# Two token tiles as one supertile, with the first MLP layers as seven block products in place of eight

## Chip, cores and metric

The kernel runs on one NeuronCore of one Trainium2 chip. The metric is the device time of one execution in microseconds (us). The figure to compare is the median of several runs.

## What is computed

The input x has 64 sequences of 64 tokens, 512 wide: 4096 tokens. Two layers follow each other. Cut to what matters:

```python
# layer 0: attention inside a sequence, then two MLPs of hidden width 2048
q, k, v  = x @ Wq, x @ Wk, x @ Wv
attn     = softmax((q @ k.T) * 512 ** -0.5)
attn_out = (attn @ v) @ Wp + bp
cms_out  = gelu(attn_out @ cW1 + cb1) @ cW2 + cb2 + one_hot(target)
modifier = gelu(concat([attn_out, cms_out]) @ mW1 + mb1) @ mW2 + mb2
x        = clip(x + cms_out + modifier, 0, 1)
# layer 1: an adapter 512 -> 256 -> 512, its weights chosen by the role of the sequence
y   = x + gelu(x @ W_down[role] + b_down[role]) @ W_up[role] + b_up[role]
out = layernorm(y) * gamma[role] + beta[role]
```

`cW1` is 512 x 2048, `mW1` 1024 x 2048, `cW2` and `mW2` are 2048 x 512. All is float32.

## The kernel before

**Numbers.** Every float32 operand of a large product is split in two fp32r parts, hi (a rounding, made by ACT) and lo (what is left, made by DVE). One product of 128 x 128 weights with 512 columns is then three matmuls: hi x hi, hi x lo and lo x hi (`mm3`, lines 1132 to 1134). So everything that PE multiplies must first pass ACT and then DVE.

**Start.** Wq Wk^T and Wv Wp are multiplied once, into eight blocks of weights. A tile's queries are then x times the first product, and the attended rows (before attention is complete they are called y) times the second give attn_out.

**Tiles.** The tokens go in eight tiles of 512. A tile has a stage A (queries of the next tile or attended rows: `project`, 4 x 4 x 3 matmuls each), a stage C (the `c` MLP) and a stage M (the `m` MLP). In C and M a loop goes over the 16 blocks `j` of 128 hidden rows: `half_step` multiplies one block of the first layer into one of the two banks `hb`, ACT takes gelu out of it twice (lines 569, 570), DVE makes the low half (line 879), and one step later `second_layer` adds the block to the four banks `acc`. The first layer takes 16 x 4 x 3 = 192 matmuls in C, 384 in M; the second 192 in each.

**Attention.** A tile has four pieces of 128 tokens (two sequences each). The steps of one piece are `scores`, the sums and the maximum of a row (`row_max`, lines 815 to 820), exp on ACT (line 530), the inverse and `p_norm` (lines 824, 826), `turn_p` (a transpose, line 1232), the split of it (lines 540, 835) and of the piece's keys `xk` (lines 536, 830), `values` (lines 1246, 1247), the sum over hi and lo (`y_sb`, line 840) and the split of y (lines 545, 846). For the next tile these steps are spread over the 16 steps of stage M, one step of a piece after each block `j`, four blocks to a piece. Only for tile 0 do they stand together: there the matmuls of Wv Wp (`product2`, 12 per piece) lie between them.

**Order.** Each engine has its own queue, written out by hand; the queues meet at counting semaphores only. An engine that waits lets nothing pass it. SP issues the weight loads, one block of 256 KB at a time into rings of `w1_st` (4) and `w2_st` (2). POOL issues x, xk and the store of z (line 448, once a tile). The weights of layer 1 are loaded and split under the last stage M (lines 601, 922). The last stage takes 34 pairs of sequences with the same role; the last tile's sequences come late in that order (`LATE`), since their z is stored last.

## Time and profile before

| | us |
|---|---|
| three runs | 2171.19, 2176.46, 2174.29 (median 2174.29) |
| the profiled execution | 2170.89 |
| its span, first to last instruction | 2169.0 |
| PE busy, of 9948 matmuls | 2140.1 |
| PE weight loads | 1780.6 |
| DVE busy | 1066.2 |
| ACT busy | 1045.0 |
| mean granted clock of PE | 0.997 of full |

The profile shows one execution. Busy time of PE is counted from a matmul's start to its modelled end, and matmuls overlap, so the spacing of starts is the price of one, not its duration (0.39 us for 512 columns). DVE and ACT overlap their operations a little too: the spacing of two starts in a full queue is below the duration. "Idle before, <-" names what ended a wait.

### The profile page before, as it was taken

The page shows a single profiled execution, that of the slowest core. Times are in us where ns is not written, and L with a number is a line of the kernel's source. Part 1 is how long each engine was busy: PE and PEld are TensorE (multiplying, and loading weights), DVE is VectorE, ACT ScalarE, POOL GpSimd, SP SyncE. Part 2 cuts the span into 40 slices and gives each one's busy share as a digit, 9 for nine tenths or more (in the row PEclk, how much of TensorE's full clock was granted, in tenths as well). Part 3 has the DMA queues.
Part 4 walks back from the last instruction along what each step waited for, and adds up shares of the span by engine and source line. Part 5 has one row for each costly group of instructions (what it writes and reads, how often), then busy time and mean ns, then how long its engine had stood idle before and what let it go on. Part 6 is the DMA issues. An engine that isn't in the chain of part 4 may idle for free.

```text
span 2169.0 us, 30587 instructions
## 1 busy us (share of the span) xinstructions
PE 2140.1 (99%) x9948; PEld 1780.6 (82%) x9949; DVE 1066.2 (49%) x1919; ACT 1045.0 (48%) x1929; POOL 75.4 (3%) x141
## 2 busy tenths in 40 slices
PE   7999999999999999999999999999999999999997
PEld 6788888888888888888888888888888888888886
DVE  6545444454435445454445445454545444354687
ACT  5545444454444545454445444454444444444564
POOL 1000000000000000000000000000000000000132
PEclk9999999999999999999999999999999999999999
...
DMA packets 126935, 247.84 MB, mean 114 GB/s; under 512 B 16653, under 2 KB 25360, under 8 KB 124112
## 3 DMA queue, kind: packets, MB, share of 16 engines
...
q14 instruction: 48, 0.39, 0.1%
...
## 4 chain that ended last, share of the span: by engine, by line
PE 95%; SPq 2%; issue 1%; DVE 1%; ACT 1%; DMA 0%; POOL 0%; ACTq 0%; POOLq 0%; DVEq 0%
PE hb L1132 19%; PE hb L1134 19%; PE hb L1133 19%; PE acc L1132 11%; PE acc L1134 11%; PE acc L1133 11%; PE scores L1224 1%; PE yb L1246 1%; SPq L356 1%; SPq L357 1%; SPq L365 0%; SPq L362 0%; PE yb L1247 0%; PE scores L1223 0%; PE acc L1378 0%
## 5 line engine op out<-in xcount | busy, mean ns | idle before, releaser
L879 DVE TENSOR_TENSOR h_lo<-hf,h_hi 128x512 fp32r<-128x512 f32 x256 | 177.2, 692 | 527.6 <-ACT hf L570 527.6
L569 ACT ACTIVATE h_hi<-hb,bias_sb 128x512 fp32r<-128x512 f32 x256 | 176.4, 689 | 483.7 <-PE hb L1134 483.6
L1132 PE MATMUL hb<-a_hi,w_hi 128*128 128x512 f32 x1024 | 403.9, 394 | 0.0
L1132 PE MATMUL acc<-h_hi,w_hi 128*128 128x512 f32 x1024 | 401.0, 392 | 0.2 <-DVE h_lo L879 0.2
L1134 PE MATMUL hb<-a_hi,w_lo 128*128 128x512 f32 x1024 | 399.5, 390 | 0.0
L1134 PE MATMUL acc<-h_hi,w_lo 128*128 128x512 f32 x1024 | 399.2, 390 | 0.0
L1133 PE MATMUL hb<-a_lo,w_hi 128*128 128x512 f32 x1024 | 398.9, 390 | 0.0
L1133 PE MATMUL acc<-h_lo,w_hi 128*128 128x512 f32 x1024 | 398.6, 389 | 0.0
L802 DVE TENSOR_TENSOR w_lo<-w_st,w_hi 128x512 fp32r<-128x512 f32 x256 | 177.1, 692 | 322.5 <-ACT w_hi L516 322.5
L516 ACT CAST w_hi<-w_st 128x512 fp32r<-128x512 f32 x254 | 157.8, 621 | 358.5 <-PE acc L1134 358.5
L797 DVE TENSOR_TENSOR w_lo<-w_st,w_hi 128x512 fp32r<-128x512 f32 x448 | 296.3, 686 | 17.0 <-ACT w_hi L511 14.0
L511 ACT CAST w_hi<-w_st 128x512 fp32r<-128x512 f32 x448 | 262.8, 618 | 9.1 <-issue 8.4
L1134 PEld LDWEIGHTS hb<-a_hi,w_lo 128*128 128x128 f32 x1024 | 192.3, 188 | 41.1
L1134 PEld LDWEIGHTS acc<-h_hi,w_lo 128*128 128x128 f32 x1024 | 192.3, 188 | 40.5
L1132 PEld LDWEIGHTS hb<-a_hi,w_hi 128*128 128x128 f32 x1024 | 192.4, 188 | 39.9
L1132 PEld LDWEIGHTS acc<-h_hi,w_hi 128*128 128x128 f32 x1024 | 192.2, 188 | 39.7 <-DVE h_lo L879 1.0
L1133 PEld LDWEIGHTS acc<-h_lo,w_hi 128*128 128x128 f32 x1024 | 192.4, 188 | 39.1
L1133 PEld LDWEIGHTS hb<-a_lo,w_hi 128*128 128x128 f32 x1024 | 192.5, 188 | 37.6
L1132 PE MATMUL hb<-c_hi,w_hi 128*128 128x512 f32 x512 | 199.7, 390 | 0.2 <-DVE c_lo L955 0.2
L1133 PE MATMUL hb<-c_lo,w_hi 128*128 128x512 f32 x512 | 199.4, 389 | 0.0
L1134 PE MATMUL hb<-c_hi,w_lo 128*128 128x512 f32 x512 | 199.4, 389 | 0.0
L570 ACT ACTIVATE hf<-hb,bias_sb 128x512 f32<-128x512 f32 x256 | 174.4, 681 | 0.0
...
## 6 DMA issues: line engine op xcount, KB each, us to landing
w_st<-w1m SPq DMA_DIRECT2D x256, 256.0 KB, 2.8
w_st<-w1c SPq DMA_DIRECT2D x128, 256.0 KB, 2.8
w_st<-w2c SPq DMA_DIRECT2D x128, 256.0 KB, 2.7
w_st<-w2m SPq DMA_DIRECT2D x128, 256.0 KB, 2.6
...
xr<-xT POOLq DMA_DIRECT2D x8, 1024.0 KB, 5.6
```

What stands on the lines that cost most here:

```text
L356: b = sp.value_load(table[0:1, bass.ds(n, 1)], min_val=0, max_val=B - 1)
L357: sp.dma_start(zs[:, slot, k, :, :].rearrange("p c s -> p (c s)"), z_dram[bass.ds(b, 1)].rearrange("o p f -> (o p) f")).then_inc(zl[slot], 16)
L511: nc.scalar.copy(w1_hi[:, k % W1_RING, :], w1_st[:, k % W1_STAGE, :]).then_inc(w1_hi_s, 1)
L516: nc.scalar.copy(w2_hi[:, k % W2_RING, :], w2_st[:, k % W2_RING, :]).then_inc(w2_hi_s, 1)
L569: nc.scalar.activation(h_hi[:, j % 2, :], hb[j % 2][:], ACT.Gelu, bias=bcol(col + j))
L570: nc.scalar.activation(hf[:, j % 2, :], hb[j % 2][:], ACT.Gelu, bias=bcol(col + j)).then_inc(h_hi_s, 1)
L797: nc.vector.tensor_tensor(w1_lo[:, k % W1_RING, :], w1_st[:, k % W1_STAGE, :], f32(w1_hi[:, k % W1_RING, :]), ALU.subtract).then_inc(w1_lo ...
L802: nc.vector.tensor_tensor(w2_lo[:, k % W2_RING, :], w2_st[:, k % W2_RING, :], f32(w2_hi[:, k % W2_RING, :]), ALU.subtract).then_inc(w2_lo_ ...
L879: nc.vector.tensor_tensor(h_lo[:, j % 2, :], hf[:, j % 2, :], f32(h_hi[:, j % 2, :]), ALU.subtract).then_inc(h_lo_s, 1)
L1132: nc.tensor.matmul(ps, w[0], x[0], start=first, stop=False)
L1133: nc.tensor.matmul(ps, w[0], x[1], start=False, stop=False)
L1134: return nc.tensor.matmul(ps, w[1], x[0], start=False, stop=last)
```

## The change

Two tiles of 512 tokens (1 and 2 of the program's names) become a **supertile** of 1024; there are four. Weights of both MLPs are loaded, split and used once per supertile. The whole order is written out; before, seven of eight tiles were a loop.

**Seven products.** Take the first layer as a product of 2 x 2 blocks: the weights by hidden half and input half, the input by input half and tile. The four blocks of the result need eight block products, or seven by the scheme of Strassen and Winograd: each of the seven multiplies a *form* (a sum or difference) of weight blocks by a form of input blocks, and sums of the products give the four blocks. A **quad** `Q` is 2 hidden blocks x 2 tiles; there are 8 in a stage (`NQ`). Its seven products `P1` to `P7` have 2 x 3 matmuls each in stage C and 4 x 3 in M. P2 is added to P1's bank, P4 to P7's and P3 to P5's by PE itself; P4 and P3 wait until DVE has read those banks.

**New work.** Per quad DVE makes four sums of weight blocks (`weight_sums`), seven low halves of weights (`split_q`), five sums of products (`sum_p6`, `sum_p7`, `block22`, `block21`, `block12`), four low halves of gelu (`hidden_lo`), and four additions into `f2` (`part`). The `part`s are there because PSUM has eight banks: four hold the second layer of tile 1 (`TB`), four hold the products (`GB`), and the second layer of tile 2 uses the product banks at a quad's end and is added up in SBUF. Per stage, 14 forms of the input are built from eight blocks: eight differences (`difference`) and splits (`form`). In stage C they are `a_forms`, in stage M both `a_forms` and `c_forms`. cms_out goes out to DRAM and comes back (`cf_dram`, `z_cms`), for want of room.

**Attention** no longer lies under stage M. It stands alone at the head of each supertile: eight pieces in a row, with one `project` (12 matmuls) between two pieces, first the queries of tile 2, then the attended rows of tile 1. The attended rows of tile 2 (`attended2`) follow the last piece.

**Layer 1's weights**: `split_l1` waits for the last P3; the load of `wu` waits for the split of `wd`. `LATE` covers two tiles.

The core of the diff (DVE's `weight_sums` and `quad`, then PE's `attention` and quads):

```diff
+NQ = JH // 2
+OB = (0, 2, 1, 3)
+
+
+P1, P5, P7, P6, P2, P4, P3 = range(7)
+
+FORM = (0, 2, 4, 5, 1, 3, 6)
+
+BANK = (0, 3, 2, 1, 0, 2, 3)
+
+RHS = {P1: (0, 2), P2: (1, 3), P3: (4, 8), P5: (5, 9), P7: (6, 10), P6: (7, 11), P4: (12, 13)}
+NF = 14
...
+            def weight_sums(Q):
+
+                cols = width(Q // NQ)
+                a11, a12, a21, a22, s3, s2, s4 = [wr[:, k, cols] for k in range(7)]
+                dve.wait_ge(raw_in, raw_done(Q))
+                nc.vector.tensor_tensor(s3, a11, a21, ALU.subtract).then_inc(sums_s, 1)
+                nc.vector.tensor_tensor(a21, a21, a22, ALU.add).then_inc(sums_s, 1)
+                dve.wait_ge(sums_s, 4 * Q + 2)
+                nc.vector.tensor_tensor(s2, a21, a11, ALU.subtract).then_inc(sums_s, 1)
+                dve.wait_ge(sums_s, 4 * Q + 3)
+                nc.vector.tensor_tensor(s4, a12, s2, ALU.subtract).then_inc(sums_s, 1)
...
+            def quad(Q):
+
+                q = Q % NQ
+                if q >= 2:
+                    part(Q - 2, 3)
+                if q:
+                    for j in range(2):
+                        split_w2(Q - 1, j)
+                if q == 0:
+                    sum_p6(Q)
+                    sum_p7(Q)
+                    block22(Q)
+                split_q(Q, P3)
+                if (Q + 1) % NQ or Q // NQ % 2 == 0:
+                    weight_sums(Q + 1)
+                if q:
+                    hidden_lo(Q - 1, C22)
+                    hidden_lo(Q - 1, C12)
+                split_next(Q, 0)
+                if q:
+                    sum_p6(Q)
+                    sum_p7(Q)
+                    block22(Q)
+                split_next(Q, 1)
+                split_next(Q, 2)
+                block21(Q)
+                hidden_lo(Q, C11)
+                split_next(Q, 3)
+                block12(Q)
+                hidden_lo(Q, C21)
+                split_next(Q, 4)
+                split_next(Q, 5)
+                if q:
+                    for i in range(3):
+                        part(Q - 1, i)
...
+            def attention(s):
+                m0 = 2 * NP * s
+                for c in range(DC):
+                    query(s, c)
+                scores(m0)
+                between(s, 0)
+                for m in range(2 * NP):
+                    turn_p(m0 + m)
+                    if m + 1 < 2 * NP:
+                        scores(m0 + m + 1)
+                    if m == NP - 1:
+                        values(m0 + m)
+                    between(s, m + 1)
+                    if m != NP - 1:
+                        values(m0 + m)
+                    if s == 0 and m == 1:
+                        sort_counts()
+                    if s == 0 and m == 4:
+                        sort_gather()
+                for j in range(DC):
+                    attended2(s, j)
+
...
+            def product(Q, k, js):
+                g = Q // NQ
+                nk = 4 if g % 2 else 2
+                bank, w = GB[g % 2][BANK[k]], ring_q(Q, k)
+                first = k in (P1, P5, P7, P6)
+                for j in js:
+                    x = forms[j // 2]
+                    i = RHS[k][j % 2]
+                    ins = mm3(bank[:], ring(w, j), (x[:, i, 0, :], x[:, i, 1, :]), first and j == 0, j == nk - 1, not first)
+                if js[-1] == nk - 1:
+                    ins.then_inc(prod[k], 1)
+
+            def quad(Q):
+
+                g, q = divmod(Q, NQ)
+                js = range(4 if g % 2 else 2)
+                old = Q - 1
+                for k, seen in ((P1, (gelu_s, 4 * old + C11 + 1)), (P5, (sum_s, 5 * old + 5)),
+                                (P7, (sum_s, 5 * old + 4)), (P6, (sum_s, 5 * old + 1))):
+                    pe.wait_ge(w1_lo_s, ring_q(Q, k) + 1)
+                    if q == 1:
+                        pe.wait_ge(*seen)
+                    else:
+                        pe.wait_ge(part_s, 4 * (Q - 2) + BANK[k] + 1)
+                    product(Q, k, js)
+                second1(old)
+                add_products(Q, js)
+                second2(old, Q)
...
+            def add_products(Q, js):
+
+                for k, seen in ((P2, (p1_s, Q + 1)), (P4, (sum_s, 5 * Q + 2)), (P3, (sum_s, 5 * Q + 3))):
+                    pe.wait_ge(w1_lo_s, ring_q(Q, k) + 1)
+                    pe.wait_ge(*seen)
+                    product(Q, k, js)
...
+            def second2(Q, Q_now):
+
+                g = Q // NQ
+                pe.wait_ge(hlo_s, 4 * Q + 4)
+                seen = ((gelu_s, 4 * Q_now + C11 + 1), (sum_s, 5 * Q_now + 1), (sum_s, 5 * Q_now + 4), (sum_s, 5 * Q_now + 5))
+                for j in range(2):
+                    for i in range(4):
+                        if j == 0 and Q_now != Q:
+                            pe.wait_ge(*seen[i])
+                        elif j == 0:
+                            pe.wait_ge(part_s, 4 * (Q - 1) + i + 1)
+                        ins = second_layer(GB[g % 2][i], j, OB[i], (h2_hi[:, j, :], h2_lo[:, j, :]), j == 0, j == 1)
+                        if j:
+                            ins.then_inc(t2_mm, 1)
+                    if j == 0:
+                        ins.then_inc(t2_half, 1)
+
+            def first_quad_c(s):
+                Q, g = 2 * NQ * s, 2 * s
+                pe.wait_ge(w1_lo_s, ring_q(Q, P1) + 1)
+                form_ready(g, 2)
```

**Order of the instructions.** First PE, around the values of a piece. Before (in the loop, stage M; `hb` is the first layer's bank, `acc` the second layer's):

```order
L1132 MATMUL hb<-c_hi,w_hi 128x512
L1133 MATMUL hb<-c_lo,w_hi 128x512
L1134 MATMUL hb<-c_hi,w_lo 128x512
L1240 REGISTER_ALU [waits xk_lo_split,pt_lo_ready]
L1246 MATMUL yb<-pt_hi_lo,xk_hi 128x256 [waits y_lo_ready]
L1247 MATMUL yb<-pt_hi_lo,xk_lo 128x128
L1246 MATMUL yb<-pt_hi_lo,xk_hi 128x256
L1247 MATMUL yb<-pt_hi_lo,xk_lo 128x128
L1206 REGISTER_ALU
L1132 MATMUL acc<-h_hi,w_hi 128x512 [waits h_lo_ready]
```


After, piece 3 of the first supertile, from its transpose (`p_norm`) to the first attended row of tile 1 (x and y are the two sets of four banks):

```order
L1614 MATMUL x<-ident,p_norm 128x128 [waits p_normalised]
L1626 MATMUL x<-pt_hi_lo,xk_hi 128x256 [waits y_lo_ready,xk_lo_split,pt_lo_ready]
L1627 MATMUL x<-pt_hi_lo,xk_lo 128x128
L1626 MATMUL x<-pt_hi_lo,xk_hi 128x256
L1627 MATMUL x<-pt_hi_lo,xk_lo 128x128
L1626 MATMUL x<-pt_hi_lo,xk_hi 128x256 [waits y_lo_ready]
L1627 MATMUL x<-pt_hi_lo,xk_lo 128x128
L1626 MATMUL x<-pt_hi_lo,xk_hi 128x256
L1627 MATMUL x<-pt_hi_lo,xk_lo 128x128
L1508 MATMUL y<-x_hi_lo,w_hi 128x512 [waits w1_lo_split,y_lo_ready,a_t1_f32,form_lo]
```


The first-layer matmuls ahead of the values and the second layer behind them are gone; transpose, values and the next projection follow each other directly, each with a wait.

DVE in attention, before, one piece of tile 0 (L840 sums y, L835 and L830 split pt and xk, L815 to L820 row sums and maximum):

```order
L846 TENSOR_TENSOR y_lo<-y_sb,y_hi 128x2x128 [waits y_hi_ready] x2
L824 RECIPROCAL rinv<-rs 128x1 [waits exp_done]
L826 TENSOR_SCALAR p_norm<-p_exp,rinv 128x128 [waits row_inverse]
L840 TENSOR_REDUCE y_sb<-yb 128x256 [waits y_mm]
L840 TENSOR_REDUCE y_sb<-hb 128x256 [waits y_mm]
L835 TENSOR_TENSOR pt_hi_lo<-scores,pt_hi_lo 128x128 [waits pt_hi_ready]
L830 TENSOR_TENSOR xk_lo<-xk_st,xk_hi 128x512 [waits xk_hi_split]
L815 TENSOR_REDUCE s_sb<-hb 64x64 [waits scores_mm]
L815 TENSOR_REDUCE s_sb<-hb 64x64
L818 TENSOR_REDUCE mx<-s_sb 128x1 [waits scores_summed]
```


After, between pieces 4 and 5 of the first supertile (L1222 the low half of an attended row, L1202 sums y, L1009 to L1014 the weight sums, L1196 and L1191 pt and xk, L1176 row sums):

```order
L1187 TENSOR_SCALAR p_norm<-p_exp,rinv 128x128 [waits row_inverse]
L1222 SCALAR_TENSOR_TENSOR a_forms<-y,bias_sb,a_forms 128x512 [waits a_t1_f32,form_hi]
L1202 TENSOR_REDUCE y_sb<-x 128x256 [waits y_mm] x2
L1009 TENSOR_TENSOR w_blocks<-w_blocks 128x256 [waits blocks_loaded]
L1010 TENSOR_TENSOR w_blocks<-w_blocks 128x256
L1012 TENSOR_TENSOR w_blocks<-w_blocks 128x256 [waits weight_sums]
L1014 TENSOR_TENSOR w_blocks<-w_blocks 128x256 [waits weight_sums]
L1196 TENSOR_TENSOR pt_hi_lo<-x,pt_hi_lo 128x128 [waits pt_hi_ready]
L1191 TENSOR_TENSOR xk_lo<-xk_st,xk_hi 128x512 [waits xk_hi_split]
L1176 TENSOR_REDUCE s_sb<-x 64x64 [waits scores_mm]
L1176 TENSOR_REDUCE s_sb<-x 64x64
```


One low half and, in this piece, four weight sums now stand in the queue ahead of pt, xk and the row sums.

DVE in the MLP, before, two steps of stage C in the loop (L797 and L802 weights, L807 x, L879 the low half of gelu):

```order
L807 TENSOR_TENSOR x_hi_lo<-x_st,x_hi_lo 128x512 [waits x_hi_split]
L796 REGISTER_ALU
L797 TENSOR_TENSOR w_lo<-w_st,w_hi 128x512 [waits w1_hi_split]
L878 REGISTER_ALU
L879 TENSOR_TENSOR h_lo<-hf,h_hi 128x512 [waits h_hi_ready]
L801 REGISTER_ALU
L802 TENSOR_TENSOR w_lo<-w_st,w_hi 128x512 [waits w2_hi_split]
L806 REGISTER_ALU
```


After, the second half of a quad's queue in stage C and the start of the next (L982 a weight form, L1086 and L1090 `block21` and `block12`, L1061 the low half of gelu, L1035 `part`, L1018 w2):

```order
L1035 TENSOR_TENSOR f<-x,f 128x512 [waits t2_part_added,t2_part_mm] x4
L1018 TENSOR_TENSOR w_lo<-w_st,w_hi 128x512 [waits w2_hi_split] x2
L982 TENSOR_TENSOR w_lo<-w_blocks,w_hi 128x256 [waits w1_hi_split]
L1009 TENSOR_TENSOR w_blocks<-w_blocks 128x256 [waits blocks_loaded]
L1010 TENSOR_TENSOR w_blocks<-w_blocks 128x256
L1012 TENSOR_TENSOR w_blocks<-w_blocks 128x256 [waits weight_sums]
L1014 TENSOR_TENSOR w_blocks<-w_blocks 128x256 [waits weight_sums]
L1061 TENSOR_TENSOR h_lo<-f,h_hi 128x512 [waits gelu_ready] x2
L982 TENSOR_TENSOR w_lo<-w_blocks,w_hi 128x256 [waits w1_hi_split]
L1067 TENSOR_TENSOR p_copy<-p_copy,x 128x512 [waits product_mm_p6,p1_copied]
L1076 TENSOR_TENSOR f<-p_copy,x 128x512 [waits gelu_ready,product_mm_p7,block_sums]
L1081 TENSOR_TENSOR f<-f,x 128x512 [waits product_mm_p5,block_sums]
```


The fourth `part` of a quad is the first thing of a later quad's queue; it waits for the last matmul of the second layer.

## Rows read from the trace of the kernel before

**Rows 1.** The page: busy tenths of PE and its granted clock in 40 slices

```profile
PE   7999999999999999999999999999999999999997
...
PEclk9999999999999999999999999999999999999999
```

**Rows 2.** Timeline of PE, first projections (start us, us, engine, line, operation, idle before)

```profile
22.70 0.47 PE L1132 MATMUL hb<-x_hi_lo,w_hi 128*128 128x512 f32 x1 [2.14 <-DVE w_lo L797]
...
24.15 0.39 PE L1132 MATMUL hb<-x_hi_lo,w_hi 128*128 128x512 f32 x1
...
33.45 0.39 PE L1134 MATMUL hb<-x_hi_lo,w_lo 128*128 128x512 f32 x1
```

**Rows 3.** The store of z, one per tile: POOL line 448

```profile
L448 POOL DMA_DIRECT2D z_by_batch<-zb x7: 907/907/922, 327.5 to 1814.1; - x7
```

**Rows 4.** Timeline of PE, attention pieces of the first tile

```profile
43.60 0.29 PE L1232 MATMUL hb<-ident,p_norm 128*128 128x128 f32 x1
...
52.92 0.29 PE L1232 MATMUL hb<-ident,p_norm 128*128 128x128 f32 x1
55.70 0.55 PE L1246 MATMUL yb<-pt_hi_lo,xk_hi 128*128 128x256 f32 x1 [2.49 <-DVE y_lo L846]
...
58.90 0.77 PE L1132 MATMUL hb<-y_hi,w_hi 128*128 128x512 f32 x1 [1.26 <-DVE y_lo L846]
```

**Rows 5.** Timeline of DVE, the same stretch

```profile
43.34 0.69 DVE L840 TENSOR_REDUCE y_sb<-yb 128x256 f32<-128x512 f32 x1
...
44.87 0.69 DVE L830 TENSOR_TENSOR xk_lo<-xk_st,xk_hi 128x512 fp32r<-128x512 f32 x1
45.48 0.58 DVE L815 TENSOR_REDUCE s_sb<-scores 64x64 f32<-64x128 f32 x2
...
46.42 0.75 DVE L846 TENSOR_TENSOR y_lo<-y_sb,y_hi 128x256 fp32r<-128x256 f32 x2
47.46 0.17 DVE L824 RECIPROCAL rinv<-rs 128x1 f32<-128x1 f32 x1 [0.29 <-ACT p_exp L530]
...
47.99 0.69 DVE L840 TENSOR_REDUCE y_sb<-yb 128x256 f32<-128x512 f32 x1
...
57.14 0.69 DVE L840 TENSOR_REDUCE y_sb<-yb 128x256 f32<-128x512 f32 x1
...
58.34 0.98 DVE L846 TENSOR_TENSOR y_lo<-y_sb,y_hi 128x256 fp32r<-128x256 f32 x2
```

**Rows 6.** Timeline of all engines, the last query of tile 0

```profile
33.87 0.58 ACT L634 CAST t_hi<-hb 128x512 fp32r<-128x512 f32 x1 [1.09 <-PE hb L1134]
...
34.49 0.69 DVE L864 TENSOR_TENSOR t_lo<-hb,t_hi 128x512 fp32r<-128x512 f32 x1 [0.83 <-ACT t_hi L634]
...
35.24 0.33 PE L1223 MATMUL scores<-x_hi_lo,t_lo 128*128 128x128 f32 x1 [0.72 <-DVE t_lo L864]
```

**Rows 7.** Windows: length, busy us (and count) of PE, PEld, DVE, ACT, POOL, clock, DMA, GB/s

```profile
21.00:22.00 1.00, 0.00 (x0) 0.00 (x0) 0.13 (x1) 0.97 (x3) 0.00 (x0) 1.00 0.04 3
...
61.00:62.00 1.00, 1.00 (x3) 0.74 (x3) 0.00 (x0) 0.00 (x0) 0.00 (x0) 0.50 0.87 221
62.00:63.00 1.00, 1.00 (x5) 0.84 (x4) 0.00 (x0) 0.00 (x0) 0.00 (x0) 0.84 0.70 195
```

**Rows 8.** Timeline of DVE, stages A and C of a tile

```profile
322.11 0.75 DVE L870 SCALAR_TENSOR_TENSOR a_lo<-hb,bias_sb,a_hi 128x512 fp32r<-128x512 f32 x1 [0.24 <-ACT a_hi L562]
...
326.02 0.76 DVE L971 TENSOR_SCALAR zb<-zt 128x512 f32<-128x512 f32 x2
```

**Rows 9.** Groups by line: the splits of the adapter's weights

```profile
L922 DVE TENSOR_TENSOR wu_lo<-l_st,wu_hi 128x1024 fp32r<-128x1024 f32 x3 | 3.7, 1227 | 0.8 <-ACT wu_hi L601 0.8
...
L601 ACT CAST wu_hi<-l_st 128x1024 fp32r<-128x1024 f32 x3 | 3.1, 1047 | 0.0
```

**Rows 10.** DMA issues: count, KB each, us to landing

```profile
x_st<-xT POOLq DMA_DIRECT2D x8, 1024.0 KB, 7.6
...
l_st<-wu POOLq DMA_DIRECT2D x1, 1536.0 KB, 7.1
```

1697 lines of the change are left out of this document (994 added, 703 removed).

## Prediction

> **What bounds the kernel now.** I read the page first. Its forty slices show PE at nine tenths everywhere but in the first and last slice, with the clock granted in full: the span is PE's own work [rows 1]. The timeline of PE gives the price of that work: from 24.15 to 33.45 us there are 41 steps of a 512-column matmul, 0.2268 us each [rows 2]. The period of the tile loop checks it: the stores of z start 1486.6 us apart over six tiles, 247.8 us a tile [rows 3]. A tile has 1056 such matmuls (48 for the queries, 48 for the attended rows, 960 in the MLPs), 239.5 us; its four attention pieces cost 1.94 us each on PE (a piece with twelve 512-column matmuls inside takes 4.66 us, half the 9.32 us between the transposes at 43.60 and 52.92 [rows 4], less 2.72). Together 247.3 us, so the loop loses 0.5 us a tile. Nothing but fewer matmuls, or a cheaper start or end, can make this faster. And every place where PE waits in the new program is a loss that the old one doesn't have.
>
> **What is removed.** Per supertile the first layers were 2 x 576 matmuls; now they are 8 x 7 x 2 x 3 = 336 in stage C and 8 x 7 x 4 x 3 = 672 in stage M. 144 fewer, 576 over four supertiles, by 0.2268 us: **130.6 us off**, all of it on the path. Weight blocks are also loaded and split once per supertile; that relieves SP, ACT and DVE, which bound nothing, so it counts nothing.
>
> **The quads.** I walked one quad of stage C by its queues. PE: 42 matmuls for the seven products and 48 for the second layer, 20.4 us. DVE: 15 operations of 512 columns, spaced by 0.61 us (44.87 to 45.48), and 11 of 256 columns at 0.34 us (two in the 0.75 us at 46.42) [rows 5]: 12.9 us, with waits inside the sums about 14. The tightest wait is P5's: it needs the fourth partial sum in f2, which DVE can start only when the last second-layer matmul is done. That add ends about 0.95 us into the quad, P5 wants its bank at 1.36. In stage M PE has 29.9 us (84 + 48 matmuls) and DVE 26 operations, 16 us. I cost the inner quads at nothing; their cover is PE's queue of products, and if DVE is 0.5 us later than I think, P5 stalls.
>
> **Attention is now uncovered.** Before, seven of eight tiles spread their pieces through stage M, where 180 matmuls lie between one piece and the next. Now eight pieces per supertile stand in a row, with twelve matmuls between. The start of the old kernel is the same pattern, with DVE already nearly full: from the first sum of y at 43.34 to the next at 47.99 its queue takes 4.65 us, and 2.51 us of that is the way from the row sums at 45.48 to the normalised p at 47.99 [rows 5]. The new queue has one operation more in each piece, the low half of a query or of an attended row: 0.61 + 1.53 (two sums and pt, 43.34 to 44.87) + 0.61 (xk) + 2.51 = 5.3 us against PE's 4.66. What else stands in the queue adds in full. I take from [rows 5, 8] (0.75 us for the biased low half, 0.38 us for a clip): piece 0, 4.7 us (PE's); piece 1 with the four sums of z2, 5.3 + 2.4 = 7.7; piece 2 with a weight split and a clip 6.3; piece 4, whose low half waits 1.4 us for two ACT passes, 6.0; piece 5 with the weight sums and a clip 7.2; piece 6 with a split 5.7. Piece 3 turns from the first tile to the second: its values wait for DVE until 3.7 us, then softmax of the next piece stands ahead of its own sums until 6.2, the first y_lo is 1.7 us behind (57.14 on DVE to 58.90 on PE) [rows 4, 5], then come the twelve matmuls: 10.6 us. Piece 7 has nothing behind it: 3.2 us to xk_lo, 0.9 us for y_lo of piece 6 and the values, 1.7 to its own y_lo: 5.8. (The old kernel's last piece took 5.98 us, 52.92 to 58.90 [rows 4].) Sum 54.0 us; PE's own work there is 8 x 4.66 less one scores and one projection, 33.6. Stall 20.4 us. Ahead of the first scores PE waits for the last query's low half, 1.5 us (the projection's last slot ends at 33.68, t_lo at 35.18 [rows 6]), and 0.3 for a split of x behind it. So 22.2 us a supertile; in the first, some 40 small linked operations of the sorting, 0.2 us each (0.17 us for one [rows 5]), take the place of z2 and clips: 27. Four supertiles: **94 us**. Bounds: 51, if DVE's operations beside each other cost nothing and only pieces 3, 7 and the start stall; 130, if each operation's full 0.69 us counts.
>
> **The clock.** The row: PE stood still for 2.49 and 1.26 us around the old kernel's last piece, and the granted clock was still 0.50 from 61 to 62 us, with the 256-column matmul at 55.70 already slow, and 0.84 in the next slice; at 21 to 22 us, in a gap of 2.14 us, it stayed at 1.00 [rows 2, 4, 7]. So one such pair of gaps cost: eight matmuls at 0.43 instead of 0.23 us and eight small ones, 2.5 us. Pieces 3 and 7 have gaps of 2.7 to 3.3 us each. Eight events, 20 us, of which I take **18**, since slow matmuls are free where DVE is late anyway; bounds 0 and 30. The Trainium skill (TensorE: Matmul & The Clock Gate, "HAM oscillation") says that a stream of matmuls with gaps goes back to the half clock again and again, burst by burst. That rule speaks against this change; its result is a rival below.
>
> **Between stages.** Attention to C: P2 waits 1.0 us for P1's copy, which stands on ACT behind the forms, P4 waits 1.6 us for the fourteen forms and two sums on DVE, and the next quad's P1 and P5 wait 1.9 us for gelu and block12: 4.5 us. C to M: the tail's second layer follows the last one at once, so its w2 low half, behind part 3, is 1.55 us late; cms, forms, parts and differences are 30 operations at 0.61 us, 18.3 us from 7.2 us on, against PE's own 19 us of products that don't need the last of them; P4 waits 1.6, the next P1 0.3: 3.4 us. M to attention: again the tail's 1.6; x, rest, z1 and the first part end at 12.4 us, as PE does. POOL's queue gets x, z_rest and both z_cms there, four transfers of 1 MB, then the next tile's xk and x. The old x took 7.6 us to land beside another [rows 10]; at twice that z_cms is still there before DVE asks for it, 11 us after the last product, and z_cms2 has 30 us. SP's stores of cms go out behind their sums, and the first difference that overwrites them comes 8 us later. Nothing for both; if the cover goes, a transfer's lateness counts in full, which is why the upper bound is high. Sum 9.5 us, four times: **38 us** (15 to 70).
>
> **The end.** The adapter's weights were split under the last stage M. Now wd waits for the last product and wu is loaded only when wd is split: 7.1 us to land [rows 10], three casts of 1.05 us and three low halves of 1.23 us overlapping [rows 9], then z; PE's tail ends at 12.4 and the first down product can start at 19.9. 7.5 us, a slow clock after it 1.5, and 3 us more of z work on DVE among the first pairs: **12 us** (6 to 20).
>
> **Given back.** The old start lost 9.1 us: gaps of 2.1, 0.7, 2.5 and 1.3 us [rows 2, 4, 6] and 2.5 for the slow clock. Of the new start all but 1.5 us (the wait for the second weight product's copy) is in the 94, so 8 in round numbers; and 0.5 us in each of seven tiles, 3.5: **-11.5 us**.
>
> **Sum.** -130.6 + 94 + 18 + 38 + 12 - 11.5 = +19.9 us on the profiled execution's 2170.9: 2190.8. The median of the runs is 3.4 us above that execution, so **2194 us**, 0.9% slower. From one kernel to another a difference of about 0.2%, 4 us, can be told.
>
> **Rivals.** (1) **The cover holds; faster.** Place: DVE's queue in the attention phase. If its extra operations slip into the 0.3 us holes and beside each other, the pieces keep PE's 4.66 us, and only pieces 3 (6.0), 7 (4.9) and the start (1.8) stall: 12.7 x 4 = 51 us, no slow clock. 51 + 38 + 12 - 11.5 - 130.6 = -41: 2133 us. For it: in the old start the same chain had PE without a gap through three pieces. Against it: DVE was full there. It decides from 23 us a supertile, stalls and clock together; above that the kernel is slower. Since my sum has 28, a part of the miss of any term is enough: 0.31. (2) **DVE becomes the bound in the quads.** Place: P5's wait on part 3. If each of 64 quads loses 0.9 us, 2194 + 58 = 2252. For it: a margin of 0.4 us. Against it: in stage M the margin is 1.8. 0.12. (3) **The slow clock stays through attention,** as the rule would have it. PE's 37 us there double; 20 of the stalls are swallowed: 17 us more a supertile, less the 18 already counted: +50, 2244. Against it: the old start, with gaps, came back to full clock after 6.6 us. 0.05. (4) My forecast, with its own range 2175 to 2225: 0.52.
>
> Rivals 2 and 3 and most of my own case are slower: 0.61; within 0.2%: 0.07; faster: 0.32. The range reaches to rival 1 but leaves out its lower half and the far ends of 2 and 3: 2133 to 2235.
>
> **What would show it.** PE's matmuls must be 576 fewer at the same 0.227 us spacing. The piece period in attention should be 5.3 to 7.7 us, with two stretches of 10.6 and 5.8; four dips in the PE row of slices, one per supertile, with the clock at 0.50 in them; DVE's releasers at scores, values and attended rows in the list of waits. Inner quads should take 20.4 and 29.9 us. I am wrong if attention takes under 49 us from the fourth query to the first attended row of tile 2, or if quads are longer than their matmuls.

## The result and the profile after

| | before | after |
|---|---|---|
| runs, median (range), us | 2173.70 (2171.19 to 2176.46) | 2219.51 (2216.09 to 2221.49) |
| ratio, 95% interval | | 1.0211 (1.0199 to 1.0223) |
| span of the profiled execution, us | 2169.0 | 2219.1 |
| granted clock of PE, mean | 0.997 | 0.969 |
| PE busy, us and records | 2140.1, 9948 | 2069.4, 9372 |
| DVE busy, us | 1066.2 | 1462.3 |

The changed kernel is 2.1% slower: 45.8 us on the medians, 50.1 us on the two profiled executions. The forecast was 20. PE has exactly the 576 matmul records fewer that were forecast. Two executions of later runs, one each of the third and the twelfth experiment, ran at a mean granted clock of 0.67 and 0.74 and took 2901.8 and 2618.8 us; they are left out of the medians below.

The page of the changed kernel, the rows that answer to [rows 1]:

```profile
PE   8689999999789999999879999999879999999797
...
PEclk9789999999889999999989999999989999999999
```

One dip per supertile, as forecast. The timeline of PE in the attention pieces of the second supertile answers to [rows 4]; a piece begins with the transpose of p (L1614), and L1626 are its values:

```profile
567.93 0.33 PE L1614 MATMUL x<-ident,p_norm 128*128 128x128 f32 x1
574.52 0.36 PE L1626 MATMUL x<-pt_hi_lo,xk_hi 128*128 128x256 f32 x1 [2.61 <-DVE y_hi_lo L1210]
575.53 0.38 PE L1614 MATMUL x<-ident,p_norm 128*128 128x128 f32 x1
581.82 0.28 PE L1614 MATMUL x<-ident,p_norm 128*128 128x128 f32 x1
586.81 0.55 PE L1626 MATMUL x<-pt_hi_lo,xk_hi 128*128 128x256 f32 x1 [3.11 <-DVE y_hi_lo L1210]
589.96 0.77 PE L1508 MATMUL y<-y_hi_lo,w_hi 128*128 128x512 f32 x1 [1.21 <-DVE y_hi_lo L1210]
594.10 0.27 PE L1614 MATMUL x<-ident,p_norm 128*128 128x128 f32 x1
...
619.70 0.36 PE L1626 MATMUL x<-pt_hi_lo,xk_hi 128*128 128x256 f32 x1 [3.97 <-DVE x_hi_lo L1210]
622.53 0.77 PE L1508 MATMUL y<-x_hi_lo,w_hi 128*128 128x512 f32 x1 [1.21 <-DVE x_hi_lo L1210]
```

Start to start, pieces 0 to 7 of this supertile take 4.77, 7.60, 6.29, 12.28, 5.88, 8.65, 6.81 and 7.09 us. Each gap shown ends on a low half that DVE writes. One more long wait, 1.08 us ahead of the transpose of piece 5, ends on p, which DVE writes too.

The windows of the same supertile answer to [rows 7] (length, then busy us and count of PE, PEld, DVE, ACT, POOL, the granted clock, DMA share, GB/s):

```profile
559.00:562.00 3.00, 3.00 (x8) 2.32 (x9) 1.07 (x5) 0.88 (x4) 0.37 (x1) 0.50 0.68 238
576.00:579.00 3.00, 3.00 (x12) 2.71 (x12) 3.00 (x7) 1.72 (x5) 0.00 (x0) 0.50 0.00 0
586.00:593.00 7.00, 4.98 (x16) 4.23 (x17) 3.56 (x10) 1.68 (x6) 0.22 (x1) 0.52 0.54 179
607.00:613.00 6.00, 6.00 (x23) 5.52 (x24) 4.72 (x14) 3.71 (x10) 0.00 (x0) 0.50 0.60 187
621.00:627.00 6.00, 4.79 (x13) 3.68 (x13) 1.65 (x4) 0.81 (x2) 0.00 (x0) 0.51 0.00 0
650.00:652.00 2.00, 1.60 (x5) 1.30 (x6) 1.71 (x4) 2.00 (x6) 0.00 (x0) 0.69 0.00 0
```

This is the first surprise: at the slice width of the page there is one dip, but in the windows PE is at 1.2 GHz in five stretches of attention and once more after it, where the forecast had two. Between them it is back at 1.00, for example from 562.5 to 574 us.

The list of PE's waits (us in total, times, longest):

```profile
PE x L1626 <- DVE x_hi_lo L1210: 29.5, 8, 5.2
PE x L1626 <- DVE y_hi_lo L1210: 26.1, 10, 5.7
PE x L1508 <- ACT f L660: 8.2, 4, 2.1
PE y L1809 <- DVE z_lo L1385: 8.1, 1, 8.1
...
PE y L1508 <- DVE f L1076: 6.9, 4, 1.9
PE x L1508 <- DVE f L1076: 6.7, 4, 1.7
PE x L1508 <- DVE w_lo L1018: 5.9, 4, 1.5
PE y L1508 <- DVE w_lo L1018: 5.9, 4, 1.5
```

**The ledger.** From the timeline of PE, stage by stage, what it needed beyond its own matmuls (0.2268 us for one of 512 columns):

| term of the sum | forecast | measured |
|---|---|---|
| 576 matmuls | -130.6 | -130.6 |
| attention, with its slow clock | 94 + 18 | 130.6 |
| attention to C | 18 | 28.2 |
| C to M, and the tails | 20 | 21.2 |
| end | 12 | 16.1 |
| given back (by difference) | -11.5 | -15.4 |
| sum | +19.9 | +50.1 |

### The profile page after: what moved, and what is told of

The parts are those of the page before. It is cut to its first block, busy times and chain, and to the rows that moved or that the text cites. A ratio compares the mean times of both kernels' runs of the same rounds, so it can differ in the third digit from the quotient of the medians.

```text
span 2219.1 us, 28615 instructions
## 1 busy us (share of the span) xinstructions
PE 2069.4 (93%) x9372; PEld 1708.4 (77%) x9373; DVE 1462.3 (66%) x2733; ACT 962.9 (43%) x1921; POOL 76.8 (3%) x144
## 4 chain that ended last, share of the span: by engine, by line
PE 81%; DVE 10%; SPq 3%; ACT 3%; issue 2%; DMA 0%; DVEq 0%; POOL 0%; ACTq 0%; POOLq 0%
PE y L1508 17%; PE y L1510 17%; PE y L1509 17%; PE x L1508 10%; PE x L1510 10%; PE x L1509 10%; DVE y_sb L1202 1%; SPq L407 1%; SPq L408 1%; DVE xk_lo L1191 1%; PE x L1626 1%; DVE a_forms L1125 1%; ACT p_exp L704 1%; DVE f L1120 1%; DVE s_sb L1176 1%
## 5 line engine op out<-in xcount | busy, mean ns | idle before, releaser
L982 DVE TENSOR_TENSOR w_lo<-w_blocks,w_hi 128x512 fp32r<-128x512 f32 (+1 forms) x476 | 255.0, 560 | 79.8 <-ACT w_hi L602 79.8
L602 ACT CAST w_hi<-w_blocks 128x512 fp32r<-128x512 f32 (+1 forms) x476 | 236.6, 515 | 139.5 <-PE y L1510 85.4
L1508 PE MATMUL y<-h_hi,w_hi 128*128 128x512 f32 x512 | 199.5, 390 | 5.9 <-DVE w_lo L1018 5.9
L1508 PE MATMUL x<-h_hi,w_hi 128*128 128x512 f32 x512 | 199.5, 390 | 5.9 <-DVE w_lo L1018 5.9
L1510 PE MATMUL y<-h_hi,w_lo 128*128 128x512 f32 x512 | 199.2, 389 | 0.0
L1510 PE MATMUL x<-h_hi,w_lo 128*128 128x512 f32 x512 | 199.2, 389 | 0.0
L1508 PE MATMUL x<-a_forms,w_hi 128*128 128x512 f32 x448 | 177.7, 397 | 18.5 <-ACT f L660 8.2
L1508 PE MATMUL y<-a_forms,w_hi 128*128 128x512 f32 x448 | 174.7, 390 | 6.9 <-DVE f L1076 6.9
L1061 DVE TENSOR_TENSOR h_lo<-f,h_hi 128x512 fp32r<-128x512 f32 x256 | 171.5, 687 | 12.5 <-ACT f L660 12.1
L1509 PE MATMUL x<-a_forms,w_hi 128*128 128x512 f32 x448 | 176.8, 395 | 0.0
L1508 PE MATMUL y<-c_forms,w_hi 128*128 128x512 f32 x448 | 174.3, 389 | 0.0
L1509 PE MATMUL y<-a_forms,w_hi 128*128 128x512 f32 x448 | 174.3, 389 | 0.0
L1509 PE MATMUL y<-c_forms,w_hi 128*128 128x512 f32 x448 | 174.3, 389 | 0.0
L636 ACT CAST w_hi<-w_st 128x512 fp32r<-128x512 f32 x128 | 78.7, 621 | 215.4 <-PE y L1510 118.8
L1086 DVE TENSOR_TENSOR f<-p_copy,y 128x512 f32<-128x512 f32 x32 | 22.0, 687 | 193.1 <-PE y L1510 193.1
```

Of the source, the lines that this page charges most:

```text
L602: nc.scalar.copy(w1_hi[:, w % RING, cols], src).then_inc(w1_hi_s, 1)
L636: nc.scalar.copy(w2_hi[:, j, :], w2_st[:, j, :]).then_inc(w2_hi_s, 1)
L982: nc.vector.tensor_tensor(w1_lo[:, w % RING, cols], src, f32(w1_hi[:, w % RING, cols]), ALU.subtract).then_inc(w1_lo_s, 1)
L1061: nc.vector.tensor_tensor(lo, half_f32(gi), f32(hi), ALU.subtract).then_inc(hlo_s, 1)
L1508: nc.tensor.matmul(ps, w[0], x[0], start=first, stop=False, skip_group_check=more)
L1509: nc.tensor.matmul(ps, w[0], x[1], start=False, stop=False, skip_group_check=more)
```

## The experiments

The runs compare with the changed kernel's 2219.5 us; the kernel before, run beside them, had a median between 2171.7 and 2173.6.

**Is it the clock?** The edit, in PE's program; at each place n matmuls into the unused bank Y[3]:

```
+ for _ in range(n):
+     nc.tensor.matmul(Y[3][:], ones2[:], t1[:, 0, 0, :], start=True, stop=True)
```

> Clock theory: what attention lost beyond the forecast is the slow clock. In the second supertile PE falls to 0.50 in five stretches of the attention phase (559 to 562, 576 to 579, 586 to 593, 607 to 613 and 621 to 627 us), where the forecast had two; busy time times missing clock is 11.5 us there. So 512-column matmuls into an unused bank, 55 a supertile in the places where PE now stands still (9 ahead of values 1, 11 ahead of values 3, 14 ahead of values 7, and so on), should keep the clock up and take 25 to 45 us off, to 2175 to 2195 us. Rival, the queue theory: DVE's queue sets the length of the pieces and slow matmuls are free beside it. Then the time changes by less than 5 us in either direction.

Measured: 2197.99 us, 21.5 less; the clock rose from 0.969 to 0.989. (The first supertile has 66 fillers, the others 55.) The gain is just short of the 25 to 45 of the clock theory and far over the 5 of its rival. Work that computes nothing made the kernel faster. In the fourth supertile, the timeline of PE:

```profile
1568.74 0.33 PE L1614 MATMUL x<-ident,p_norm 128*128 128x128 f32 x1
1573.85 0.35 PE L1626 MATMUL x<-pt_hi_lo,xk_hi 128*128 128x256 f32 x1 [1.10 <-DVE y_hi_lo L1210]
1574.87 0.33 PE L1614 MATMUL x<-ident,p_norm 128*128 128x128 f32 x1
...
1583.19 0.47 PE L1508 MATMUL y<-y_hi_lo,w_hi 128*128 128x512 f32 x1 [0.35 <-DVE y_hi_lo L1210]
1586.02 0.28 PE L1614 MATMUL x<-ident,p_norm 128*128 128x128 f32 x1
```

Piece 3 fell from 12.79 to 11.15 us, the 48 matmuls of the second tile's attended rows from 13.7 to 11.0 us. Pieces 1 and 2 are 7.60 and 6.13 us as before, but in this supertile no slow stretch had fallen into them. In the second supertile one had fallen into piece 2 (576 to 579 us), and piece 2 went only from 6.29 to 6.13 us: there the queue theory is right that slow matmuls are nearly free beside DVE.

> The fillers of the first experiment, five to ten more a supertile where PE still stood still, and new ones ahead of the first scores (4) and at the three waits of stage C's first two quads (3, 6, 7). Clock theory: attention to stage C is 7.0 us over its matmuls, of which only 4.6 are waits as forecast, and the rest is a last dip of the clock: 2 us a supertile here and 1 to 2 in attention: 8 to 14 us under the first experiment's 2198, so 2184 to 2190, with a mean clock over 0.995. Rival: the first fillers took all that the clock was worth: within 4 us of 2198.

Measured: 2191.15 us, mean clock 0.995, 6.8 under the first filler run (forecast 8 to 14). This is the changed kernel with the clock up but for two dips of 3.4 us in attention, so it splits the ledger. (It has 91 fillers a supertile, 95 in the first.) From the end of the fourth query to P2 of the second quad of stage C the four supertiles took 433.6 us after the change and 404.0 here: 29.6 less, 3.1 on the way to the first transpose, 11.6 in the pieces, 9.6 in the attended rows of tile 2, and 5.3 in stage C.

> The changed kernel with fillers only at the three waits of stage C's first two quads (3, 6 and 7 matmuls, four times). Attention to stage C took 7.0 us over its matmuls where 4.5 were forecast; its three waits are 4.6. If the rest is the clock falling in these waits, 2.4 us come back four times: 8 to 10 us less, 2210 to 2212. Rival: the fall stems from attention and is over before, or the fillers delay what they fill: 3 us less or nothing.

Measured: 2213.84 us, 5.7 less by the medians, 7.6 by the spans. The stretch from stage C's first product to P2 of its second quad fell by the same 5.3 us as in the run before, so this part of the clock's price is made in that place. It is less than the 8 to 10 expected, since a wait costs more than its row says. With the clock up, this stretch still loses 5.7 us a supertile against the 4.6 us of idle time in the changed kernel's rows. From start to start, each wait costs 0.24 us more than its idle: the record ahead of it lasts 0.39 us for a spacing of 0.23, and the first step behind it is 0.31 (645.58 to 645.89 us in this run). That is 0.7 for the three, and a fourth, short wait of 0.3 follows them.

**Is it where DVE's operations stand, or how many there are?** The edit:

```
  values(m), PE:
-     pe.wait_ge(y_lo_s, m * 2 - 1 + h)
+     pe.wait_ge(y_sum, m * 2 - 1 + h)
  sum_y(m, h), DVE:
+     if m: dve.wait_ge(y_lo_s, m * 2 - 1 + h)
```

> Values of a piece wait until DVE has written the low half of the piece before, although their bank is free as soon as the sum is taken; that low half stands behind the row maxima of the next piece in DVE's queue. Here they wait for the sum alone. Place theory: it is where this wait stands in the queue, not how much DVE does, that makes the 2.6, 2.9 and part of the 3.1 and 4.0 us gaps ahead of values in a supertile. Then the time falls by 20 to 45 us. Rival, the work theory: DVE has too much to do in each piece, and what values win the next transpose of p loses: 0 to 8 us less.

Measured: 2219.77 us, nothing. The place theory fell. The timeline of PE shows the wait changing its name, not its end:

```profile
567.76 0.33 PE L1616 MATMUL x<-ident,p_norm 128*128 128x128 f32 x1
573.02 0.36 PE L1628 MATMUL x<-pt_hi_lo,xk_hi 128*128 128x256 f32 x1 [1.25 <-DVE pt_hi_lo L1196]
575.36 0.33 PE L1616 MATMUL x<-ident,p_norm 128*128 128x128 f32 x1 [1.23 <-DVE p_norm L1187]
```

Values come 1.3 us sooner after the piece's start, and the transpose behind them waits 1.23 us for p. The piece is 7.60 us, as it was. (Pieces 5 and 7 did fall, from 8.65 to 7.93 us and from 7.09 to 6.32; over the four supertiles the pieces took 3.6 us less, and the ways to the first transposes and the attended rows of tile 2, where the clock fell more, took 2.9 more.) The 55.6 us that the list of waits puts on DVE's low halves are DVE's work, wherever the wait stands.

The order in piece 3, and the clips. The edit on DVE:

```
  piece m == NP - 1:
+ split_y(m - 1) ahead of row_max(m + 1)
+ sum_y(m), split_y(m) ahead of normalise_p(m + 1)
+ z2_clip(s - 1, 0..3) behind it
- z2_clip(s - 1, m - 1) in pieces 1 to 4
```

> Two moves in DVE's queue alone: in piece 3 the low half of piece 2 goes ahead of the row maxima, and the sums and low halves of piece 3 go ahead of the normalising of piece 4; and the four clips of z2 leave pieces 1 to 4 for the 5.3 us in which DVE stands still behind piece 3. By the queue's lengths: 1.7 us in each of four supertiles and 1.5 us in three, 11 us less; with a dip of the clock that is shortened by it, 15. Rival: what leaves one piece is absorbed by the next wait: 3 us less or nothing.

Measured: 2212.07 us, 7.4 less, where 11 to 15 were expected. Piece 3 went from 12.5 to 11.5 us, piece 5 from 8.65 to 7.60, pieces 1 and 2 stayed: the clips that left them were not what their waits ended on.

So I took out the rest of what is not the pieces' own chain:

```
+ z2_sum(s - 1, 0..3): around the first two queries
  piece 3, behind normalise_p(4):
+ z2_clip(s - 1, 0..3), weight_sums(Q), split_q(Q, 0), split_q(Q, 1)
+ in the first supertile sort_halves(), sort_slots()
- all of these in pieces 0 to 6
```

ACT's casts for the two weight splits go along.

> What DVE does in attention beside the chain of the pieces goes where it stands still: z2's sums (2.49 us in piece 1) into the query phase, the clips (1.5), the weight sums (1.4) and two weight splits (1.2), and in the first supertile the middle of the sorting (4.4), into the 5.3 us behind piece 3. Work theory: pieces 1 to 6 fall to 5.1 to 5.5 us; 2.5 + 1.5 + 1.4 + 1.2 = 6.6 us less in three supertiles and some 4 in the first, 24 us, and as gaps become shorter, fewer dips of the clock: another 5 to 12. 2184 to 2196. Rival, the chain theory: a piece is as long as the chain from p to p (maxima, exponential, normalising), not as DVE's work: 8 us less or nothing.

Measured: 2194.62 us, 24.9 less, just inside the range. No engine does less; the work only stands where DVE was idle (5.3 us behind piece 3, 1.1 to 2.3 us between queries). The timeline of PE, second supertile:

```profile
560.92 0.33 PE L1626 MATMUL x<-ident,p_norm 128*128 128x128 f32 x1
...
566.12 0.33 PE L1626 MATMUL x<-ident,p_norm 128*128 128x128 f32 x1
...
595.61 0.33 PE L1626 MATMUL x<-ident,p_norm 128*128 128x128 f32 x1
...
601.61 0.33 PE L1626 MATMUL x<-ident,p_norm 128*128 128x128 f32 x1
```

Piece 1 is 5.20 us (7.60 after the change), pieces 5 and 6 are 6.00 (8.65 and 6.81). The work theory holds; the chain theory falls.

> The low half of each xk block is taken by GpSimd in place of DVE: one operation of 0.61 us less in each of eight pieces of DVE's queue. Since relaxing the wait of values moved nothing (the next transpose of p came no sooner: pieces of 7.60 us stayed at 7.60), the work theory says that DVE's queue is full: 0.6 us less in each of pieces 1 to 7, 4.3 us a supertile, 17 us in all, and up to 25 with shorter dips of the clock: 2195 to 2202. Rival: GpSimd's subtraction is so slow, or slows DVE's operations beside it so much, that values wait for it instead: no gain, or a loss of up to 20 us.

Measured: 2213.28 us, 6.2 less: between the two. Pieces 4, 5 and 6 fell as the work theory says (5.30, 7.41 and 6.07 us, 0.6 to 1.2 less), pieces 1 and 2 did not move. There GpSimd gets in DVE's way. In piece 1 its subtraction runs from 568.68 to 569.97 us; DVE's first sum of z2 starts at 569.11 and ends at 570.51, 0.54 us behind it. The tile view of z's cms, z2's sums on DVE (duration min, median, max), first of the changed kernel, then of this run:

```profile
L1259 DVE TENSOR_TENSOR f<-f,z_cms x16: 681/684/686, 569.8 to 2082.2; 128x512 f32<-128x512 f32 x16
```

```profile
L1266 DVE TENSOR_TENSOR f<-f,z_cms x16: 675/679/1405, 569.1 to 2075.9; 128x512 f32<-128x512 f32 x16
```

In each of the three supertiles with sums of z2 in attention the first of the four takes 1.40 us: 0.72 us more, as much as the operation taken away. In piece 2 it is the low half of a weight block (0.68 to 1.40 us, beside GpSimd from 576.40 to 577.68). The Trainium skill (SBUF — State Buffer, "Who interferes with whom") has this: an operation of DVE with two inputs in SBUF contends with one of GpSimd that reads SBUF, and the ports that the two share are an exclusive lock. The trace agrees: DVE's operation ends some 0.55 us behind GpSimd's, both times. Two sums of y, which read PSUM, took 1.28 us beside the same subtraction and 1.28 without it.

**The tails.** The edit: in the last second layer of a stage, `split_w2(Q, 0)` ahead of `part(Q - 1, 3)` on DVE.

> In the last second layer of each stage the low half of the first weight block goes ahead of the fourth partial sum on DVE. The forecast charged 1.55 us to this order at eight places: the time falls by 12 us, to 2207. Rival: the fourth partial sum, now later by 0.6 us, or the second block's half then holds PE instead: 3 us less or nothing.

Measured: 2216.96 us, 2.6 less. The forecast of 12 failed, and by the time alone, a difference under the 4 us that can be told, the rival stands. The trace shows what moved. The wait was 1.47 us at eight places in the changed kernel, and here, by the timeline of PE:

```profile
288.25 0.47 PE L1508 MATMUL y<-h_hi,w_hi 128*128 128x512 f32 x1 [0.80 <-DVE w_lo L1018]
```

0.67 us less each, 5.4 in all; part of it went again where the clock fell (the ways from the fourth query to the first transpose took 1.7 us more). The forecast named the fourth partial sum as what the half stands behind. It also stands behind the first three, which are queued ahead of that; the high half is done at 285.44 us in this run, the low half starts at 287.42. In the combined kernel below it goes ahead of all four, and the tail ends 1.75 us sooner after the last product (16.32 against 18.07).

**Are the quads PE's alone?** The edit: `product(Q, P1, js)` is issued twice.

> In all quads but the first of each stage the product P1 is taken twice (the second time from the start of its bank, so that the result is unchanged): 4 x 7 x (6 + 12) = 504 matmuls more. If PE bounds the quads with nothing else near it, as the forecast had it, each costs 0.2268 us: 114.3 us more, 2334. Rival, DVE as a near bound of the quads (P5 waiting for the fourth partial sum): the added 1.4 us ahead of P5 would cover that wait, and the time would grow by less: 100 us or under.

Measured: 2329.68 us (two executions), 110.2 more by the medians, 108.4 by the spans. The inner quads of stages C and M grew by 1.36 and 2.72 us each, all alike, which is six and twelve matmuls to the hundredth; over 28 and 28 quads that is the 114.3. The 5.9 less lie outside the quads (stage C began 1.8 us sooner in the first supertile alone). In the changed kernel they take 20.40 and 29.93 us, as forecast. So P5 waits in none of them. How near DVE comes is not a thing that this run can show, for any margin above nothing gives the same time; the trace of the changed kernel does. The fourth partial sum, then the start of the quad (P1):

```profile
691.09 2.73 DVE L1035 TENSOR_TENSOR f<-x,f 128x512 f32<-128x512 f32 x4 [1.26 <-PE x L1510]
692.92 0.39 PE L1508 MATMUL x<-a_forms,w_hi 128*128 128x512 f32 x1
```

The sums end at 693.82, 0.90 us into the quad, and P5 starts at 694.28: 0.46 us of margin in stage C, and 1.8 in M, as the forecast had it.

**The end.** Three attempts. First, wu is loaded into a buffer of its own, when the last product is done:

```
- sp.wait_ge(l1_lo, R);  dma(l1_st, wu)
+ sp.wait_ge(prod[P3], 2 * NQ * NS);  dma(wu_st, wu)
```

> At the end wu is loaded into a buffer of its own as soon as the last product is done, not behind the split of wd. Forecast term of the end (7.5 us of waiting for the first z, measured 8.1): the load is then off the chain; three casts and three low halves behind those of wd leave PE a wait of 1 to 3 us: 5 to 7 us less, 2213 to 2215. Rival: the load competes with the reads of x, cms and z that start at the same time, and the sums of z's rest that stand ahead in DVE's queue come later: 2 us less or nothing.

Measured: 2219.39 us, nothing, and PE's wait for z_lo is 8.1 us as before. The timeline of DVE in this run:

```profile
2053.46 3.50 DVE L1379 TENSOR_TENSOR wd_lo<-w_blocks,wd_hi 128x1024 fp32r<-128x1024 f32 x3 [0.25 <-ACT wd_hi L821]
2059.93 2.73 DVE L1037 TENSOR_TENSOR f<-y,f 128x512 f32<-128x512 f32 x4 [2.97 <-PE y L1512]
2062.57 2.49 DVE L1240 TENSOR_TENSOR z_rest<-z_rest,z_cms 128x512 f32<-128x512 f32 x4
2064.98 3.49 DVE L1379 TENSOR_TENSOR wu_lo<-wu_st,wu_hi 128x1024 fp32r<-128x1024 f32 x3
```

ACT made wu's high halves from 2055.23 to 2058.2; the low halves stand behind the last partial sums, which wait for PE, and z's rest. The next experiment takes z's rest to be waiting for cms. The rows show otherwise: it starts with no idle time behind the partial sums, and cms had landed by 2058.8 (issued at 2045.2 at the latest, 13.5 us to land at most). In addition, z's rest goes behind wu's low halves and behind the first two z:

> The sixth experiment took the load of wu off the chain and changed nothing: PE still waited 8.1 us for the first z, because in DVE's queue the sums of z's rest stand ahead of wu's low halves and themselves wait for cms to land (12.6 us behind the split of w2, before and after). Here wu is loaded early and the low halves of wu and of z's first two pairs go ahead of z's rest. New theory: the 8.1 us are the wait for cms, not for wu; both had to go: 5 to 7 us less than 2219.5, 2213 to 2215. Rival: the sums of z1, which the first pair's second step needs, are then late by as much: 2 us less or nothing.

Measured: 2219.49 us, nothing again. PE's wait fell to 5.65 us, by the 2.4 us of DVE's work on z's rest, and the first down product came 2.4 us sooner after the last product, but the seventh only 0.9 (53.1 us against 53.9). The low halves of wu still stood behind the last partial sums, in whose wait DVE was idle for 2.96 us. Third, in the fourteenth run below, they go ahead of these as well: PE's wait is 3.7 us, and from the last product to the end it takes 169.4 us where the changed kernel takes 176.9. Of these 7.5 us 1.75 are the tail's.

**All together.**

> The last two together, with the relaxed wait of values, the order in piece 3, the first w2 low half of each tail ahead of the partial sums (1.47 us at eight places, of which 0.67 went in the fourth experiment), the last attended row of the first tile behind the last values (it covers the 2.4 us of the last low half), and fewer fillers (35 a supertile in attention, 16 around the first quads of stage C, 4 ahead of the scores). Sum of the parts as measured or forecast: clock 28, extras 24, piece 3 and clips 6, tails 12, end 6, last row 6: 82 less if they add, 2137. I expect two thirds of it, 2160 to 2170, below the kernel before. Rival: the parts share the same waits, and it stays above 2174.

The last attended row moves so, on PE, and ACT and DVE follow:

```
- piece 6: turn_p, scores, attended1(3), values;  piece 7: turn_p, values
+ piece 6: turn_p, scores, values;  piece 7: turn_p, values, attended1(3)
```

(The fillers in attention were 33 in the first supertile and 29 in the others, not 35.) Measured: 2158.65 us, ratio 0.9933 (0.9916 to 0.9950) to the kernel before: faster than both. 60.9 of 82 us, under three quarters, and 1.4 us better than the range.

> The eleventh experiment without its fillers. Clock theory: shorter gaps still drop the clock at piece 3 and behind the last values; 10 to 20 us slower than with fillers, 2169 to 2179. Rival: with the extras gone the gaps are too short for the clock to fall, and the fillers were worth nothing here: within 4 us of 2158.7.

Measured: 2174.10 us, 15.5 more than with fillers; 1.0002 (0.9992 to 1.0012) to the kernel before. So the reordering alone brings the change to break-even, and the clock's share on top of it is still 15 to 16 us: shorter gaps drop it too.

> The eleventh experiment with fillers added where PE still stood still 0.8 to 2.5 us (ahead of the transposes of pieces 3, 6 and 7, ahead of the last values and at stage C), and with wu's low halves ahead of the last partial sums. The mean clock goes from 0.989 to over 0.995: 4 to 8 us less. The first down product comes 2 to 3 us sooner, but from the ninth experiment I expect none of it at the end. 2151 to 2155. Rival: fillers of that number now delay what they stand before: no gain.

The new order at the end, on DVE: `split_l1(1)` (wu's low halves) ahead of the last four `part(Q, i)`. Measured: 2155.21 us, 3.4 less, clock 0.995. That is under the 4 us that can be told, but the trace places it: all of it is the end, 4.0 us less from the last product on (173.4 to 169.4). Piece 6 went from 6.00 to 7.40 us in the second supertile. Its rows, first the values, then the five fillers ahead of the next transpose:

```profile
586.81 0.55 PE L1650 MATMUL x<-pt_hi_lo,xk_hi 128*128 128x256 f32 x1 [1.72 <-DVE xk_lo L1199]
588.54 2.16 PE L1666 MATMUL y<-t_hi_lo,ones 128*128 128x512 f32 x5
```

The granted clock is 0.50 from 586.8 to 590.2 us, so the fillers take 2.0 us and the transpose stands behind them. In the third and fourth supertile, where the dip is in part later, the piece takes 6.95 and 6.24 us. A filler is free only inside a wait, and costs double when the clock falls all the same.

> The fourteenth with the low half of xk on GpSimd. Pieces 4 to 6 are 5.6 to 6.0 us by DVE's queue in the eleventh; in the fifth experiment GpSimd took 0.6 us off each such piece, and beside its 1.29 us DVE's operations grew (z2's sums from 2.49 to 3.20 us). Work theory: 0.5 us in each of pieces 1, 2, 4, 5 and 6, 10 us less than the fourteenth at best; with the two engines in each other's way and xk late at the last values, 3 to 8 us less. Rival: the pieces are now set by the chain from p to p: no gain, or a loss of up to 5 us.

Measured: 2142.90 us, ratio 0.9860 (0.9845 to 0.9875) to the kernel before: 12.3 less than the fourteenth, where I had 3 to 8. In the second supertile pieces 2 to 6 went from 5.61, 9.75, 5.55, 6.00 and 7.40 us to 5.39, 9.18, 5.16, 5.87 and 4.73; the timeline of PE there:

```profile
550.52 0.29 PE L1644 MATMUL x<-ident,p_norm 128*128 128x128 f32 x1
555.90 0.29 PE L1644 MATMUL x<-ident,p_norm 128*128 128x128 f32 x1
561.29 0.27 PE L1644 MATMUL x<-ident,p_norm 128*128 128x128 f32 x1
...
570.47 0.27 PE L1644 MATMUL x<-ident,p_norm 128*128 128x128 f32 x1
575.63 0.27 PE L1644 MATMUL x<-ident,p_norm 128*128 128x128 f32 x1
581.50 0.27 PE L1644 MATMUL x<-ident,p_norm 128*128 128x128 f32 x1
...
584.04 0.36 PE L1656 MATMUL x<-pt_hi_lo,xk_hi 128*128 128x256 f32 x1 [0.66 <-POOL xk_lo L493]
...
584.98 1.38 PE L1672 MATMUL y<-t_hi_lo,ones 128*128 128x512 f32 x5
586.23 0.33 PE L1644 MATMUL x<-ident,p_norm 128*128 128x128 f32 x1
```

The same move was worth half as much alone (6.2 us). Half of the 12.3 lies in piece 6 (6.7 us over the four supertiles): PE waits 0.66 us for xk's low half in place of 1.72, the clock stays up, and the five fillers take 1.3 us in place of 2.0. Besides, z2's sums, which GpSimd had held up, no longer stand in attention; what it holds up here is one low half of y in each of pieces 3 and 7 (1.3 us in place of 0.41, in three supertiles). How much each of these adds was not tried. The page:

```profile
PE   8899999999999999999999999999999999999897
...
PEclk9999999999999999999999999999999999999999
```

## Why the prediction was right in sign and wrong in size

The forecast was +20 us and 2194; it came to +46 and 2219.5, inside the range. Point by point, by its own steps:

- **What is removed.** Right: 576 matmuls, 0.2268 us, 130.6 us, all on the path. The doubled P1 shows the price from the other side.
- **The quads.** Right: 20.40 and 29.93 us. Rival 2 falls. The margin of 0.4 us, which the forecast gave as the reason to fear it, was there as forecast (0.46 us), and it held in every inner quad.
- **The clock: the term of 18 us was mis-sized by 11.** By the second filler run it is worth 29 us. The step that failed was "Pieces 3 and 7 have gaps of 2.7 to 3.3 us each. Eight events, 20 us": I counted only the gaps as long as those of [rows 2, 4]. In the second supertile PE fell to 0.50 five times, among them behind a gap of 1.40 us with 0.39 behind it, and once more in stage C. My one row at 1.00 in a gap of 2.14 us [rows 2, 7] was a single draw. The same wait ahead of the first scores (1.40 us, then 0.39) stands in all four supertiles, and the way from the fourth query to the first transpose took 7.22, 7.45, 5.99 and 5.99 us: the clock fell in two of four. In the run with fillers in stage C alone it took 5.64, 7.43, 7.56 and 7.56. The length of the gap does not decide alone, so I should have charged each of attention's waits with a share. The rule of the Trainium skill (TensorE: Matmul & The Clock Gate, "HAM oscillation"), that PE is throttled again in the wait behind each burst, was nearer than my row, though the trace shows it behind some of the waits only. Its full result, rival 3 at 0.50 all through, did not come: between the dips the clock was back at 1.00. The forecast's "slow matmuls are free where DVE is late" held in piece 2, the one place where it can be read.
- **Attention's stalls: a term of 94 us, mis-sized by 12; 106 with the clock up** (the second filler run's 299.6 us from the fourth query to stage C, less 193.1 of PE's own). The mechanism was right: DVE's queue. In the third supertile of that run pieces 0 to 4 came to 4.8, 7.6, 6.1, 10.7 and 5.9 us against 4.7, 7.7, 6.3, 10.6 and 6.0. Pieces 5, 6 and 7 were undersized: 7.9, 6.3 and 6.8 against 7.2, 5.7 and 5.8. The first supertile, 27 forecast, was some 3.5 us longer. (The 180 matmuls that the forecast puts between two old pieces are 144 in the trace; nothing in the sum rests on them.)
- **Between stages.** 38 forecast, 49.4 measured, nearly all of the miss from attention to C. Its three waits were sized right (0.9, 1.7 and 2.05 us, 4.6 against 4.5). Left out were the clock (1.3 us a supertile) and 1.1 us for the restart behind each wait and a short fourth one. C to M and the tails came within 1.2 us of the forecast. What the tails' wait was put down to was incomplete, as the fourth experiment shows.
- **The end.** 12 forecast, 16 measured, with PE's wait 8.1 against 7.5. The size of the wait was right by luck and **its cause was wrong**: the load of wu, which the forecast put on the chain, was not what held it. Taking it away changed nothing. What held wu's low halves was DVE's queue: the last partial sums, which wait for PE's tail, and z's rest behind them (not cms, which had landed). With wu early and z's rest moved, the way from the last product to the end fell by 1.1 us; with the partial sums out of the way too, by 5.8 beside the tail's 1.75. From its first matmul on the adapter took 7.9 us longer than before, where 4.5 were forecast; 5.3 of it lie in its first six pairs, and why is left open.
- **Given back.** -11.5 against -15.4; it is a difference, and holds what the other terms left over.
- **Rival 1** (attention under 49 us in the stretch named) is out: that stretch took 65.0 to 72.9 us. Its place, DVE's queue, was the right one, and its assumption that the extra operations find room there failed. Even with the extras moved and xk on GpSimd only pieces 0 and 6 come near its 4.66 us (4.65 and 4.73); pieces 1, 2, 4 and 5 take 5.2 to 5.9.

Together: clock 11, stalls of attention 12, waits between stages 6 (without the clock), end 4, less 4 of what was given back: 29 of the 30 us between forecast and measured span.
